# Attention in column tiles of 32: every TensorE product of the stage in one tile shape, one key tile per step, and one probability tile moved from GpSimd's sum to TensorE's

## What is computed

```python
q = (x @ Wq.T).reshape(b, t, N_HEADS, HEAD_DIM)
k = (kv_latent @ Wk_up.T).reshape(b, t, N_HEADS, HEAD_DIM)
v = (kv_latent @ Wv_up.T).reshape(b, t, N_HEADS, HEAD_DIM)
scores = jnp.einsum('bqhd,bkhd->bhqk', q, k) * scale
attn = jax.nn.softmax(scores, axis=-1)
out = jnp.einsum('bhqk,bkhd->bqhd', attn, v)
```

## Time and profile before

| | us |
|---|---|
| median of 3 runs | 2265.46 |
| lowest, highest run | 2260.86, 2268.83 |
| profiled execution, span from first to last instruction | 2203.9 |
| median less that span | 61.6 |

### The profile page before, as it was taken

How to read it: one execution, slowest core, us unless ns; L and a number is a source line. 1 busy time by engine, 2 the same in 40 slices (tenths; PEclk the granted TensorE clock), 3 DMA queues, 4 the chain that set the end, 5 groups by cost and what they waited for, 6 DMA issues and landing times. The chain is left out here.

```text
span 2203.9 us, 47779 instructions
## 1 busy us (share of the span) xinstructions
PE 1734.9 (79%) x12049; PEld 979.0 (44%) x12049; DVE 1469.4 (67%) x3940; ACT 1187.6 (54%) x2321; POOL 1509.8 (69%) x1151
## 2 busy tenths in 40 slices
PE   7979999999999999996772799377777766100997
PEld 3423433444444444333662688244444444000897
DVE  5756878888788887882787244178888887620453
ACT  4626777777777777775562355234444444021343
POOL 0006999999999999995677333588888883155565
PEclk9978999999999999998555899699999998555999
DMA  5753221222212222221242233400000000132232
GB/s 157 248 173 109 62 62 58 60 60 61 64 58 60 61 60 65 58 69 55 95 142 83 94 126 126 141 20 20 19 19 19 19 19 1 43 113 98 84 105 60
DMA packets 158016, 167.97 MB, mean 76 GB/s; under 512 B 39521, under 2 KB 124392, under 8 KB 157960
## 3 DMA queue, kind: packets, MB, share of 16 engines
q1 hardware_dynamic: 143128, 137.02, 20.3%
q0 software_dynamic: 13824, 29.43, 4.2%
q10 hardware_dynamic: 1008, 0.92, 0.1%
HBM read 93.57 MB, written 73.97 MB: 76 GB/s over the span
## 5 line engine op out<-in xcount | busy, mean ns | idle before, releaser
L764 DVE TENSOR_REDUCE halfmax<-p_m 128x1 f32<-128x512 f32 x1024 | 640.4, 681 | 169.7 <-PE p_m L637 169.6
L751 ACT ACTIVATE probs<-p_s,ESCALE 128x512 f32<-128x512 f32 x1024 | 621.7, 691 | 103.1 <-PE p_s L661 100.1
L591 POOL TENSOR_TENSOR sum_p<-sum_p,probs 128x1024 f32<-128x1024 f32 x256 | 604.8, 2362 | 17.2 <-ACT probs L751 1.1
L637 PE MATMUL p_m<-ka,qa 96*128 96x512 f16 x1024 | 398.5, 391 | 14.2 <-DMA vh<-v 12.0
L661 PE MATMUL p_s<-qa,ka 98*128 98x512 f16 x1024 | 392.2, 386 | 10.3 <-ACT probs L751 4.4
L666 PE MATMUL p_o<-probs,vh 128*32 128x256 f32 x4096 | 275.6, 387 | 0.0
L1647 PE MATMUL ln_p_cum<-ln_kv,c_tri 128*128 128x512 f32 (+1 forms) x384 | 163.8, 570 | 91.6 <-POOL ln_kv L1591 91.6
L1304 ACT ACTIVATE e_h<-e_p_h,e_w 128x256 f32<-128x256 f32 x316 | 126.3, 474 | 172.8 <-PE e_p_h L1283 172.5
L661 PEld LDWEIGHTS p_s<-qa,ka 98*128 98x128 f16 x1024 | 99.5, 98 | 214.2 <-ACT probs L751 125.8
L591 POOL TENSOR_TENSOR sum_p<-probs 128x1024 f32<-128x1024 f32 x64 | 150.8, 2356 | 60.6 <-ACT probs L751 60.6
L1220 POOL DMA_INDIRECT xs<-r_xn,r_slot x128 | 125.7, 982 | 69.3 <-issue 35.1
(11 more groups left out here) (299 smaller groups left out, 2718.3 us busy)
## 6 DMA issues: line engine op xcount, KB each, us to landing
e_xb<-xs SPq DMA_DIRECT2D x40, 257.0 KB, 2.7
e_xb<-xs SPq DMA_DIRECT2D x78, 128.0 KB, 2.0
ys<-e_y SPq DMA_DIRECT2D x78, 128.0 KB, 1.9
v<-pj_v SPq DMA_DIRECT2D x8, 1024.0 KB, 4.9
qa<-q SPq DMA_DIRECT2D x64, 128.0 KB, 2.6
ka<-k SPq DMA_DIRECT2D x64, 128.0 KB, 2.7
vh<-v SPq DMA_DIRECT2D x64, 128.0 KB, 2.1
o<-ot SPq DMA_DIRECT2D x64, 128.0 KB
```

What stands on the lines that cost most here:

```text
L591: nc.gpsimd.tensor_tensor(sum_p[s % 2][:, :], (sum_p[s % 2] if n else probs[0])[:, :], probs[k][:, :], ALU.add).then_inc(sum_p_d, 1)
L637: nc.tensor.matmul(max_bank(s, n)[:, :], qa[s][0:KA, (n // 2) * P:(n // 2 + 1) * P], ka[s][0:KA, (n % 2) * HALF:(n % 2 + 1) * HALF], start ...
L751: nc.scalar.activation(probs[k][:, h * HALF:(h + 1) * HALF], score_bank(s, k, h)[:, :], ACT.Exp, scale=ESCALE[:, 0:1]).then_inc(probs_d, 1)
L764: nc.vector.reduce_max(halfmax[s % 2][:, n // 2, n % 2:n % 2 + 1], max_bank(s, n)[:, :], AX.X).then_inc(max_read, 1)
```

## The change

Three things are done, all in `attend`:

1. Every maximum and every score, one product with a weight of 128 columns before, is now four products with weights of 32 columns over the same 512 moving columns, at `tile_position=(0, 32 j)`. The turn becomes a plain f32 product with the identity at (0, 0), where it was a transposition.
2. `key_tiles` becomes `key_tile`: a step has the two scores and two maxima of one key tile and then the values of one.
3. `POOL_SUMS` loses its last tile. GpSimd makes 4 additions a head in place of 5, TensorE takes the denominators of tiles 5, 6 and 7, and ScalarE waits for the denominators of the head before ahead of `probs[5]`.

```diff
-POOL_SUMS = (1, 2, 3, 4, 5)
+POOL_SUMS = (1, 2, 3, 4)
...
             max_bank_read(pe, u, max_place(s, n))
-            nc.tensor.matmul(max_bank(s, n)[:, :], qa[s][0:KA, (n // 2) * P:(n // 2 + 1) * P],
-                             ka[s][0:KA, (n % 2) * HALF:(n % 2 + 1) * HALF], start=True, stop=True).then_inc(max_scores, 1)
+            for j in range(4):
+                mm = nc.tensor.matmul(max_bank(s, n)[j * DH0:(j + 1) * DH0, :],
+                                      qa[s][0:KA, (n // 2) * P + j * DH0:(n // 2) * P + (j + 1) * DH0],
+                                      ka[s][0:KA, (n % 2) * HALF:(n % 2 + 1) * HALF], start=True, stop=True,
+                                      tile_position=(0, j * DH0))
+            mm.then_inc(max_scores, 1)
...
-            nc.tensor.transpose(turn_bank(s)[0:KT, 0:P], rowmax[:, :], c["ident"][:, :]).then_inc(max_T, 1)
+            nc.tensor.matmul(turn_bank(s)[0:KT, 0:P], rowmax[:, :], c["ident"][:, :], start=True, stop=True,
+                             tile_position=(0, 0)).then_inc(max_T, 1)
...
-            cols, q = slice(k * P, (k + 1) * P), slice(h * HALF, (h + 1) * HALF)
-            nc.tensor.matmul(score_bank(s, k, h)[:, :], ka[s][:, cols], qa[s][:, q], start=True, stop=True).then_inc(scores, 1)
+            q = slice(h * HALF, (h + 1) * HALF)
+            for j in range(4):
+                cols = slice(k * P + j * DH0, k * P + (j + 1) * DH0)
+                mm = nc.tensor.matmul(score_bank(s, k, h)[j * DH0:(j + 1) * DH0, :], ka[s][:, cols], qa[s][:, q],
+                                      start=True, stop=True, tile_position=(0, j * DH0))
+            mm.then_inc(scores, 1)
...
+        def key_tile(pe, r, s, k):
+            nxt = (r, s, k + 2) if k + 2 < KT else (*after(r, s), k + 2 - KT)
+            for h in range(2):
+                n = 2 * k + h
+                if exists(*nxt[:2]):
+                    score(pe, *nxt, h)
+                if n == TURN and exists(r, s, 1):
+                    max_turn(pe, *after(r, s))
+                if exists(r, s, 2):
+                    max_half(pe, *after(r, s, 2), n)
+            values(pe, r, s, k)
...
-            for k in range(2, KT, 2):
-                key_tiles(pe, r, s, k)
+            for k in range(2, KT):
+                key_tile(pe, r, s, k)
             if exists(r, s, 1):
-                key_tiles(pe, *after(r, s), 0)
+                for k in range(2):
+                    key_tile(pe, *after(r, s), k)
             denominators(pe, r, s)
```

More of the change, by code:

```diff
@@ L723, in _ @@
                     score(pe, 0, 0, k, h)
-            key_tiles(pe, 0, 0, 0)
+            for k in range(2):
+                key_tile(pe, 0, 0, k)
             with pe.Fori(0, LAST) as r:
```

## The result

| | us |
|---|---|
| before, median (17 runs) | 2265.46 |
| changed kernel, median (17 runs) | 2278.62 |
| ratio, 95% interval | 1.0056 (1.0039 to 1.0072) |

The account below looks back on a forecast made before the run. TensorE was taken to set the period, 13.14 us a head; tiles, order and moved denominator gave 12.31, plus 0.1 doubt 12.41. Over 61 heads that gains 44.5 us, so 2221 us, range 2210 to 2252.

Parts of the forecast that it names:

- column tiles for all products: Scores and maxima on TensorE: each as four 32-column products costs 0.216 us instead of 0.219, a gain of 0.10 a head.
- round trips: TensorE's four passages a head between whole-array products and column-tiled values, 0.24 us each, vanish: -0.96 a head.
- one more denominator on TensorE: Two more groups of denominator products on TensorE: +0.43 us a head, while GpSimd is no longer near the bound.
- one key tile a step: waits gone: The new order in a head removes the wait behind the turn and the score-bank wait: together -0.3 us.
- doubt about the step from f16 to f32: Values groups: a slow first group, 0.02 eight times a head, may come from the type; half of 0.2 added, 0.1.
- the passage goes with the tile's shape and not with the type: Read from the projections and the turn: TensorE loses some 0.2 us when tile shape changes, nothing from f16 to f32.
- the first rival: TensorE's loop code no longer stays on the core and is refetched at branches: 21 us lost, 2242 us; 3 in 10.
- The fetch: At each branch back: 1.7 to 2.5 us for code plus the stop, less 1.7 of queued denominators; 1.5 taken.
- What lies around the span: The 61.6 us between the profiled span and the median, carried over unchanged to reach 2221 us.
- four f16 tiles: Rival for scores and maxima: tiles miss the values' pace; at 0.239 us a product the gain is gone, 2266; 1 in 10.
- the passage is not paid by type: Rival: each step pays 0.24 us for the f16-f32 change, eight times a head, +1.1 a head, 2332 us; 7 in 100.
- the new order has no wait: Rival: late rows of maxima or VectorE make waits, period 12.6 to 12.9, 2235 to 2255 us; 6 in 100.

Follow-up runs that it names:

- run 1: The changed kernel with TensorE's loop of 15 passes written out, so no branch back: 2160.88 us, ratio 0.9801 to before.
- run 7: The kernel before with only GpSimd's last addition given to TensorE: 2229.72 us, ratio 1.0111, period 13.57.
- run 9: The kernel of run 1 with the old order, four scores and four maxima ahead of two values: 2172.01 us, ratio 0.9857.
- run 11: The kernel of run 10 plus 70 instructions without effect ahead of TensorE's loop, which shift its code: 2342.77 us, ratio 1.0379.
- run 10: The changed kernel, loop kept, with each second maximum over the whole array, 1737 instructions in the loop: 2432.86 us, ratio 1.0778.
- run 2: The changed kernel with eight heads in TensorE's loop body instead of four, 6 branches back instead of 14: 2183.82 us, ratio 0.9905.
- run 5: The changed kernel itself, unchanged, measured again on a chip where before takes 2205 to 2206 us: 2212.6 us, ratio 1.0042.
- run 6: The kernel before with one key tile a step, whole-array products, five GpSimd additions and the loop kept: 2243.8 us, ratio 1.0176.

## Why the prediction was wrong

**The head's sum was right.** Forecast 12.41 us a head, of 12.31 and a doubt of 0.1; run 1 measures 12.43. Forecast gain 44.5 us; run 1 gains 44.4. By its terms:

| | forecast, us a head | measured, us a head |
|---|---|---|
| column tiles for all products (round trips -0.96, products -0.10, turn +0.10) | -0.96 | -0.91 (run 7 to 9) |
| one more denominator on TensorE | +0.43 | +0.43 (run 7) |
| one key tile a step: waits gone | -0.30 | -0.23 (run 9 to 1) |
| doubt about the step from f16 to f32 | +0.10 | not told apart |
| together | -0.73 | -0.71 |

Single readings go with it. The reading of the earlier trace rows, that the passage goes with the tile's shape and not with the type, is borne out from two sides: no gap from f16 to f32 in one shape in the timeline after, and 0.11 on the way into the whole array with f16 on both sides in run 11. What the way back costs was not seen without a change of type, but that change costs nothing in one shape. 226 records a head pass in 12.43, one in 0.055 us, over the whole stage. The weight loads did not get slower: those of 32 columns take 98 ns in the mean (L668, after), as those of 128 did (L661, before). GpSimd has 490 of 600 us in run 1, 82%, where some 85% were said.

**The step that failed is the first rival.** "The loop's code no longer stays on the core" was given 3 in 10 and "1.5 for each of 14 branches", at most 2.7. The forecast itself put the branch at nothing. What the rival says is what happened, and it costs 3.8 to 4.2 us a branch. Two terms of it were too small:

- *The fetch.* I took 1.7 to 2.5 for a transfer from the earlier trace rows and took off the denominators still queued, 1.7 us, as cover. The start-to-start gaps at the 14 branches are 2.8 to 3.5 us, 44 us in all, and 2.9 us a branch are lost where the clock stays. The branch instruction takes 3.9, so the wait for the code is longer than the small DMA in the earlier trace rows, and the denominators hide only 0.9 of it: they are partly through when the branch begins.
- *The clock behind it.* This was not in the sum at all. The earlier trace rows show 1.00, and there the array stood for 2.3 us of 600; where it stands for 3 us, the products behind the gap run at half pace for some 3.3 us, after 11 of the 14 gaps. Those eleven branches cost 4.6 us and the other three 2.9, so of the total of (13.45 - 12.43) x 58 = 59 us some 18 are the clock's, 1.3 a branch.

14 x 4.2 = 59 us exceed the 44.5 of the gain, which makes the kernel slower; my upper end of 38 could not, and so the range stopped at 2252.

**The chance was too low as well.** The earlier trace rows show that four heads of 1089 instructions are held. For 1929 the prediction counted "some 8 packets" and left open whether 8 are too many. Runs 10 and 11 show that they are: a loop that touches 7 stays, one that touches 8 is fetched whole each time, since one more packet is fetched ahead. The Trainium skill, "Runtime: NRT & Kernel Launch", section Instruction fetch mechanics, gives TensorE 128 KiB in blocks of 16 KiB; that agrees with runs 10 and 11, with the one ahead counted among the eight. By that rule the prediction made the rival as likely as the forecast, but left its own chance at 3 in 10. It did not count the packet ahead: the earlier trace rows show packets in the first pass, but not which of them is ahead. With that packet counted the case was near to certain.

**What lies around the span** was no term of the end but an assumption about it: 61.6 us carried over unchanged. It does not lie around the span. In run 1 the profiled execution takes 2162.5 us at a span of 2160.8, a difference of 1.7. The rest of the 61.6 is, as far as the record shows, the difference between two chips, most of it in the routing stage. It cancels in the ratio and did no harm.

The other rivals did not come: four f16 tiles keep 0.22 (not 0.239), the passage is not paid by type, and the new order has no wait from 300 to 900 us in run 1. The margin of 0.7 us that the prediction gave the rows of maxima is thin, though: in run 2 they are late twice, by 0.6 and 0.4 us. The times of that rival were also a little high: 61 heads of 12.6 to 12.9 give 2233 to 2251, not 2235 to 2255. What makes the routing stage of one chip take 192 us and of another 240 was not followed.

## What to carry to other kernels

Before an unrolled loop is made longer, count the packets of code that one pass touches, with the one fetched ahead: the cost is a step from nothing to several us a branch, it depends on where the loop starts, and no sum over products shows it. Writing such a loop out costs nothing where the code comes in order. A stall of the array is priced with the slow clock that can follow it, not by its own length alone; and a part that loses alone (the order, 38 us; the moved sum, 24) can be right once another part has taken away what made it cost.

## What the runs showed of the hardware

- TensorE's store of code: a loop over 7 packets of 16 KB is held, one over 8 is fetched in full, 9 packets a pass, at 3.8 to 7.6 us a branch (changed kernel, runs 5, 10 and 11). The packets of a loop are worked out by count.
- A branch whose code is held takes 0.2 us and is hidden; one whose code is not takes 3.9.
- 124 packets of code over the whole program are no load when they come in order (run 1, ratio 0.9801; before written out, 1.0002).
- Behind a stop of TensorE of 2.8 to 3.5 us the granted clock was 0.50 for some 3.3 us at 11 of 14 branches of the changed kernel, which made a branch 1.6 us dearer.
- The passage of the array between column tiles of 32 and the whole array costs 0.23 to 0.24 us there and back (runs 6 and 11); the 0.11 of the way in is paid at one type, f16, too.
- Four column tiles of 32 over the same 512 f16 columns take 0.22 us together, as one product over the whole array does (run 1).
- One kernel, before, takes 2204 to 2206 us on three chips and 2259 on a fourth. Of the 73 us between the first two profiles, which seem to be of one chip of each kind, 48 lie in the routing stage.
